# Queries and keys of an attention kernel as three bf16 terms instead of two f32r terms

## The chip, the cores and the metric

One NeuronCore of a Trainium2 chip runs one program. The metric is the device time of one execution in microseconds (us); of the kernel before, three executions are given.

## The reference

The input is x of shape 8 x 512 x 128 (batch, tokens, features), in f32. It passes two layers.

Layer 0: xn = layernorm(x), h = rmsnorm(xn). From h come q, k and v of 16 heads with 8 features each. There are two kinds of attention. The *linear* one is causal with the weight 1 + s + s²/4, where s is the product of 16 features made of q and of k; the *sliding* one is a softmax over the last 65 tokens, of q·k/sqrt(8). Their outputs, side by side, go through Wout. Beside them a feed-forward part runs on xn: silu(w1 x) * (w2 x), two hidden layers of 512 x 512 with gelu, and w3. The sum with x gives x1.

Layer 1: xn = layernorm(x1); *causal* softmax attention over the 512 tokens of a batch, 16 heads of 8 features, and beside it a choice of 2 of 8 experts for each token, each expert a 128-512-128 network with gelu, weighed by the softmax of the two logits. The sum of all is the output.

## The kernel before

**Scores.** All attention scores are made by `scores_into` (its matmul is L708): for a head and a block of 128 queries or keys, a matmul of 128 x 128 stationary against 128 to 512 moving columns. A head's keys stand in a buffer of 128 rows of which only its own rows are not zero, so the queries of several heads can lie in one 128-row block. To reach f32 precision a query and a key are each split in two f32r terms, high and low. A head takes 32 rows: three slots of 8 rows (high·high, low·high, high·low) and 8 rows of which one is used for minus the row maximum against a row of ones (the softmax shift). So 4 heads share a block of queries (`HG`), and Q1, QM, Q2 have 4 blocks of 512 tokens, K1 and K2b one block for each of 16 heads, all f32r (L298, L330). Q1 and K1 serve the sliding scores, QM and K1 the linear ones, Q2 and K2b the causal ones of layer 1.

**Splitting and moving.** ScalarE writes the high term (`split_hi`, L1111), VectorE subtracts it from the bank (`split_lo`, L1546). SyncE sends the terms to DRAM slot by slot (`split_and_send`, L516; `send`, L491), and ScalarE's queue sends those of q2 itself (L1244, L1248). From there SyncE fetches them into their slot rows (`fetch`, L498), for keys one DMA for each of the four head positions.
Row maxima are made ahead of the scores that use them: scores with queries as the stationary side, then a custom VectorE operation (`row_max`, L1579) reduces them; the table of maxima is transposed by TensorE, negated by `negate_max` (L1606) and put into the slot row by SyncE (`place_max`, L527).

**Stages.** Each batch of 512 tokens goes through a pairs stage, a slide stage and a dense stage; layers and batches are interleaved. In the pairs stage of batch b TensorE runs (`pairs_stage`, L834) the linear scores of batch b, row maxima for the causal scores of b-1 and for the sliding ones of b, the causal scores of b-1, and `weigh` (L766), the sums of values by heads, in bursts of 32 matmuls. ScalarE puts every score unit through exp or a square into `probs` (L1119), GpSimd masks them (L1308), VectorE does the maxima. A small bf16 sum over tokens, `prefix` (L826), counts the rows chosen for each expert. In the slide stage (`slide_stage`, L891) come the 32 sliding score units of b, and between them the projections of q, k and q·M for b+1 (q1, k1, qm1) and, from unit `GATES_AT` on, the 16 gate matmuls of the feed-forward part (L680). In the dense stage (`dense_stage`, L949) come the hidden layers for b+1 (`dense_low`, L701, 12 matmuls of 512 columns a unit, f32r terms high·high, low·high, high·low), and in the middle the end of layer 0 and the start of layer 1 for b: x1, its statistics, k2, q2, xnT, the expert logits and the choice.
The order on every engine is written out by hand. Seven PSUM banks are handed out in a ring; a unit waits until its bank was taken (`to_bank`), and an engine that reads a unit increments the bank's `taken` semaphore. In order of issue at the turn from layer 0 to 1: ScalarE writes high of k2, then of q2, then issues two sends of q2 (L1244), a gelu, and the third send. VectorE writes low of k2 and of q2 and then copies xnT, which TensorE's logits matmuls (L685) wait for.

**Parts.** The span has an opening (batch 0 only up to its queries and keys), batch 0 (`first`), six `steady` batches, a `last` batch without a following one, and a tail with the causal part of batch 7 and the expert tiles, which are sorted by expert (`stage_tile`, L1769, copies the weights of a tile's expert; L1782 copies its transposed input). In the opening SyncE fills the slot rows of ones (`set_slots`, `set_keys`, L482). Half of K1 and half of K2b double as room for the low parts of the hidden layers' weights and activations: SyncE loads these again from DRAM each batch (`load_low`, L512, L567 ff.) and GpSimd clears the room afterwards (`clear`, L1366, called in L1412 ff.). The expert weights W1 and W2 lie over Q1, QM and K1 (L331), so `load_experts` (L634) waits in the last batch for its last slide unit.

## Time and profile before

| | |
|---|---|
| median of three runs | 1272.86 us (1271.83 to 1275.03) |
| span of the profiled execution, first to last instruction | 1269.4 us |
| TensorE matmul (PE) busy | 1189.8 us, 94% |
| TensorE weight load (PEld) busy | 894.4 us, 70% |
| VectorE (DVE) busy | 848.0 us, 67% |
| ScalarE (ACT) busy | 734.5 us, 58% |
| GpSimd (POOL) busy | 665.2 us, 52% |
| DMA queues q1, q0, q10: packet time as a share of 16 engines | 25.2%, 5.3%, 2.0% |

A profile is of one execution; the profiled one has no device time of its own beside its span, so its span stands against the median of the runs, 3.5 us above it. The steady batch read here is that of 416.25 to 544.8 us; its pairs stage ends at about 476, its slide stage at about 509. In the rows, "PE bank L708" is a matmul of `scores_into`, "heads" one of `weigh`; K, Q, QM and W_s are names of whole groups of buffers. The chain of waits gives pieces in order of time, each followed back to what released it.

### The profile page before, as it was taken

The numbers are of one execution on the slowest core, as the hardware profiler recorded it, in microseconds if no ns is written. First come the engines' busy times: TensorE is split into PE (matmuls) and PEld (weight loads), VectorE is DVE, ScalarE is ACT, GpSimd is POOL, SyncE is SP. The second block draws the span as 40 slices with busy tenths as digits, with TensorE's granted clock in tenths as the row PEclk, the third lists the DMA queues.
The fourth block names the chain that finished last, engine by engine and source line by source line (L and its number), as shares of the span: only waits on it lengthen the run. The fifth ranks groups of instructions, "written<-read, shape, count | busy, mean of one in ns | idle before, by whom it ended". The sixth has DMA issues, their size and how long they took to land.

```text
span 1269.4 us, 26751 instructions
## 1 busy us (share of the span) xinstructions
PE 1189.8 (94%) x9122; PEld 894.4 (70%) x9122; DVE 848.0 (67%) x3390; ACT 734.5 (58%) x1561; POOL 665.2 (52%) x921
## 2 busy tenths in 40 slices
PE   5988999999999999999999999999999857989996
PEld 2566777677767776777677767776776657885896
DVE  4066597659865986588658855886588646874563
ACT  2356367736773577357745774567456524557674
POOL 4574364536443644464446444644465436675677
PEclk9999999999999999999999999999999968999999
DMA  7704420432043304230423043304330056541333
GB/s 219 210 3 162 132 77 12 158 123 92 13 160 109 106 14 159 96 120 13 158 97 119 13 151 105 117 15 137 118 117 15 11 151 147 81 66 25 45 55 39
DMA packets 88039, 119.30 MB, mean 94 GB/s; under 512 B 13736, under 2 KB 46416, under 8 KB 85904
## 3 DMA queue, kind: packets, MB, share of 16 engines
q1 hardware_dynamic: 69312, 99.66, 25.2%
q0 software_dynamic: 13792, 9.54, 5.3%
q10 hardware_dynamic: 4800, 8.39, 2.0%
q8 instruction: 73, 1.20, 0.4%
q14 instruction: 62, 0.51, 0.1%
HBM read 70.78 MB, written 48.46 MB: 94 GB/s over the span
## 4 chain that ended last, share of the span: by engine, by line
PE 63%; DVE 13%; ACT 10%; issue 6%; POOL 3%; DMA 3%; SPq 0%; DVEq 0%; POOLq 0%; ACTq 0%
PE bank L708 18%; PE heads L766 13%; PE bank L701 12%; PE bank L680 7%; ACT probs L1119 5%; PE bank L676 3%; PE bank L691 2%; DVE xnT_s L1579 2%; POOL out L1361 2%; PE bank L1054 2%; DVE hrow L1579 2%; DVE hT_s L1579 2%; PE bank L816 2%; PE bank L1062 1%; PE bank L685 1%
## 5 line engine op out<-in xcount | busy, mean ns | idle before, releaser
L1119 ACT ACTIVATE probs<-bank 128x512 f32<-128x512 f32 (+2 forms) x896 | 443.3, 578 | 186.5 <-PE bank L708 180.2
L1308 POOL TENSOR_SCALAR_AFFINE_SELECT probs<-probs 128x384 f32<-128x384 f32 x256 | 127.4, 520 | 211.7 <-ACT probs L1119 211.2
L708 PE MATMUL bank<-K,Q 128*128 128x192 f32 (+4 forms) x1024 | 236.5, 308 | 0.0
L708 PE MATMUL bank<-Q,K 128*128 128x192 f32 (+4 forms) x1024 | 220.7, 322 | 3.3 <-ACT probs L1119 3.1
L766 PE MATMUL heads<-probs,V 128*18 128x192 f32 (+9 forms) x3072 | 196.1, 396 | 6.6 <-POOL probs L1311 3.9
L708 PEld LDWEIGHTS bank<-K,Q 128*128 128x128 f32 x1024 | 166.5, 189 | 21.7 <-issue 9.6
L708 PEld LDWEIGHTS bank<-Q,K 128*128 128x128 f32 x1024 | 152.3, 194 | 39.5 <-issue 17.5
L766 PEld LDWEIGHTS heads<-probs,V 128*9 128x9 f32 (+1 forms) x3072 | 78.5, 94 | 114.0 <-issue 75.6
L1361 POOL DMA_INDIRECT out<-h1T_s x78 | 123.1, 1578 | 60.0 <-ACT h1T_s L1269 35.6
L708 PE MATMUL bank<-QM,K 128*128 128x512 f32 (+3 forms) x512 | 138.4, 336 | 4.6 <-ACT probs L1119 3.8
L1261 ACT ACTIVATE h2T_s<-bank,h1T_s 128x128 f32<-128x128 f32 x312 | 89.2, 368 | 91.8 <-PE bank L1054 88.9
L1320 POOL TENSOR_SCALAR_AFFINE_SELECT probs<-probs 128x512 f32<-128x512 f32 x64 | 54.9, 858 | 121.5 <-ACT probs L1119 121.1
L708 PEld LDWEIGHTS bank<-QM,K 128*128 128x128 f32 x512 | 85.2, 189 | 21.8 <-ACT probs L1119 6.2
L1369 POOL MEMSET K<- 128x512 f32 x120 | 57.1, 527 | 81.3 <-PE bank L701 80.9
L1054 PE MATMUL bank<-h1T_s,w_in 128*128 128x128 f32 x624 | 86.7, 284 | 0.0
L1579 DVE CUSTOM_DVE_ANT_0 hT_s<-bank,causal_neg_s 128x128 bf16<-128x128 f32 (+3 forms) x184 | 77.8, 455 | 13.1 <-PE bank L708 13.1
L1062 PE MATMUL bank<-w_out,h2T_s 128*128 128x128 f32 x624 | 83.9, 278 | 0.7 <-ACT h1T_s L1269 0.7
L1054 PEld LDWEIGHTS bank<-h1T_s,w_in 128*128 128x128 f32 x624 | 79.2, 199 | 0.8 <-issue 0.5
L1109 ACT ACTIVATE probs<-bank,sh_s 128x512 f32<-128x512 f32 x36 | 24.8, 688 | 94.8 <-PE bank L701 64.0
L1062 PEld LDWEIGHTS bank<-w_out,h2T_s 128*128 128x128 f32 x624 | 77.4, 195 | 0.8 <-ACT h2T_s L1261 0.8
L1348 POOL DMA_INDIRECT sorted_rows<-rows,slot_i x64 | 63.8, 998 | 16.5 <-issue 10.6
L1579 DVE CUSTOM_DVE_ANT_0 xnT_s<-bank,causal_neg_s 128x256 bf16<-128x256 f32 (+3 forms) x146 | 69.6, 502 | 4.0 <-PE bank L708 3.9
(224 smaller groups left out, 2184.9 us busy)
## 6 DMA issues: line engine op xcount, KB each, us to landing
Q<-slots_of_q SPq DMA_DIRECT2D x15, 1024.0 KB, 8.0
K<-low_of_h SPq DMA_DIRECT2D x13, 1024.0 KB, 7.8
QM<-slots_of_qm SPq DMA_DIRECT2D x8, 1024.0 KB, 6.0
K<-slots_of_k SPq DMA_DIRECT2D x60, 128.0 KB, 2.7
K<-slots_of_k SPq DMA_DIRECT2D x68, 96.0 KB
slots_of_q<-Q SPq DMA_DIRECT2D x24, 256.0 KB, 3.0
slots_of_k<-QM SPq DMA_DIRECT2D x24, 256.0 KB, 4.0
slots_of_qm<-Q SPq DMA_DIRECT2D x24, 256.0 KB, 4.2
```

The lines of the kernel that those rows point to most:

```text
L680: pe.matmul(to_bank(run, unit)[:, :], w, x, start=True, stop=True).then_inc(full_sem(run, unit), 1)
L701: mm = pe.matmul(to[:, :], left[:, n % FC, c * P:(c + 1) * P], right[n % FC], start=(n == 0), stop=(n == 3 * FC - 1))
L708: mm = pe.matmul(to[:, at:at + right.shape[1]], left, right, start=True, stop=True, skip_group_check=True)
L766: mm = pe.matmul(heads[ROWS * i:ROWS * i + n, P * j:P * j + widths[j]], V[:, j, g // 2, i, first:first + n], slot_of(kind, 2 * g + i // 2) ...
L1054: mm = pe.matmul(tile_hidden_bank(i)[:, c * P:(c + 1) * P], w_in[:, i % WB, c * P:(c + 1) * P], tile_xT[:, i % 2, :], start=True, stop=True)
L1062: mm = pe.matmul(tile_out_bank(i), tile_hidden[i % 2][:, c * P:(c + 1) * P], w_out[:, i % WB, c * P:(c + 1) * P], start=c == 0, stop=c == ...
L1119: return act.activation(to, bank, func, scale=scale, bias=bias).then_inc(taken_sem(run, unit), 1)
L1261: last = act.activation(tile_hidden[i % 2][:, c * P:(c + 1) * P], tile_hidden_bank(i)[:, c * P:(c + 1) * P], ACT.Gelu, bias=tile_b1[:, i % ...
L1308: pool.affine_select(out=three, in_=three, compare_op=ALU.is_ge, fill=0.0, base=0, pattern=[[0, 3], [1, P]], channel_multiplier=-1)
L1348: pool.indirect_dma_start(out=sorted_rows, out_offset=bass.IndirectOffsetOnAxis(ap=slot_i[:, n:n + 1], axis=0), in_=rows[:, n // K2, n % K ...
L1361: pool.indirect_dma_start(out=out.rearrange("b t d -> (b t) d"), out_offset=bass.IndirectOffsetOnAxis(ap=tile_rows[:, i % XB, P + 1:P + 2] ...
L1579: last = dve.tensor_tensor_reduce(beside[:, at:at + n], bank_of(run, unit)[:, at:at + n], mask, 1.0, NEG, ALU.add, ALU.max, to)
```

## The change

Queries and keys become three bf16 terms each. A head takes 64 rows: for each of 8 features six slots (pairs of terms with high·high, high·middle, middle·high, high·low, low·high, middle·middle) and two more for minus the maximum, itself now two bf16 terms. Two heads share a 128-row block (`SH`), Q1, QM and Q2 have 8 blocks in bf16, and K1 and K2b still 16, at half the bytes. After the high term (ScalarE) and the rest (VectorE, f32), ScalarE rounds the rest to the middle term (`split_mid`) and VectorE subtracts that for the low one (`split_low`). For k2 and q2 these stand in the dense stage, before VectorE's copy of xnT; for q1, k1 and qm1 in the slide stage, after unit 11 (ScalarE) and 13 (VectorE). Each term is sent by one DMA that writes it into one to three slots, and keys are fetched by two DMAs a half.
The low parts of the hidden layers stay in SBUF; their reload and GpSimd's clearing in every batch go. Expert weights lie over the unsplit gate and hidden activations (`whole_a`, `whole_b`), which are used last in the dense stage ahead of the last batch, and are loaded at the start of the last batch. The rows of ones come from a buffer of bf16 pairs, for all five at the opening.

```diff
+SG, SH = H // 2, 2
+SROWS = 64
+SLOT = 8
+AT_MAX = 6
+SLOTS_Q, SLOTS_K = ((0, 3, 1), (3, 5, 1), (5, 6, 1)), ((1, 6, 2), (0, 5, 4), (2, 3, 1))
+ONE_PAIR = 1.0 + 0x3F80 / 2 ** 23
...
-        Q2 = sb("Q2", [P, G, T], F32R)
+        Q2, K2b, K1 = sb("Q2", [P, SG, T], BF16), sb("K2", [P, H, T], BF16), sb("K1", [P, H, T], BF16)
         with ExitStack() as aside:
-            K2b = sb("K2", [P, H, T], F32R, aside)
-        whole_b = sb("whole_b", [P, H, T])[:, H // 2:H // 2 + FC, :]
+            low_a, low_h1, low_b, low_h2 = (sb(n, [P, FC, T], F32R, aside) for n in ("low_a", "low_h1", "low_b", "low_h2"))
+        W1, W2 = sb("W1_s", [P, E, T]), sb("W2_s", [P, E, FC, P])
...
+        def three(buf, first):
+            return buf[:, first, :], buf[:, first + 1, :], buf[:, first + 2, :]
+
+        def whole(buf, first):
+            return buf[:, first:first + 2, :].rearrange("p a t -> p (a t)").bitcast(F32)
+
+        parts_of = {"q1": three(Q2, 0), "qm1": three(Q2, 3), "k1": three(QM, 0), "q2": three(Q2, 0), "k2": three(Q2, 3)}
...
+        def by_slot(name):
+            return scratch[name].rearrange("h (d s) t -> (h d) s t", s=SLOT)
...
+            def set_slots(name, src):
+                sp.dma_start(by_slot(name)[:, AT_MAX:SLOT, :], src.rearrange("p (s t) -> p s t", t=T)).then_inc(S["slots_set"], 16)
...
+            def send(sequence, name, n):
+                sem = ("high", "mid", "low")[n]
+                sp.wait_ge(S[f"{sem}_{name}"], due(f"{sem}_{name}", sequence, 1))
+                sp.dma_start(slots_view(name, n), slots_src(name, n)).then_inc(S[f"sent_{name}"], 16)
...
-                    for i in range(HG):
-                        sp.dma_start(to[ROWS * i:ROWS * i + rows, HG * groups.start + i:HG * groups.stop:HG, :].bitcast(F32), by_row[i][0:rows, groups])\
+                    by_row = scratch[name].rearrange("(g i) r t -> i r g t", i=SH)
+                    for i in range(SH):
+                        sp.dma_start(to[SROWS * i:SROWS * (i + 1), SH * groups.start + i:SH * groups.stop:SH, :], by_row[i][:, groups])\
...
-                n = mrow.shape[0] // HG
-                for i in range(HG):
-                    row = ROWS * i + 3 * D
...
+                n = mrow.shape[0] // SH
+                for i in range(SH):
+                    for part in range(2):
+                        row = SROWS * i + AT_MAX + part
...
             def body(run, before, this, after):
                 part, b = run
+                if not after:
+                    load_experts()
...
                 if after:
                     for name in ("q1", "k1", "qm1"):
-                        split_and_send(run, (b, 1), name)
...
-                    load_low("h1", low_h1)
-                    if before:
-                        sp.wait_ge(taken_sem(run, CAUSAL_UNITS[-1]), taken_at(run, CAUSAL_UNITS[-1]))
-                        load_low("h2", low_h2)
-                    load_x((b, 1), (b + 2) & (NB - 1))
+                        send((b, 1), name, 0)
+                if after:
+                    for n in (1, 2):
+                        for name in ("q1", "k1", "qm1"):
+                            send((b, 1), name, n)
                 if before and this:
                     store(run, b - 1)
+                if this and after:
+                    load_x((b, 1), (b + 2) & (NB - 1))
                 if not after:
-                    load_experts(run)
...
                     sp.wait_ge(S["sent_k1"], due("sent_k1", (b, 1), SENT))
+                    fetch("k1", LOWER)
+                    fetch_sent((b, 1), "qm1")
                     fetch("k1", UPPER, "upper")
-                    fetch_sent((b, 1), "qm1")
                     fetch_sent((b, 1), "q1")
-                    if this:
-                        sp.wait_ge(S["keys1_restored"], due("keys1_restored", (b, 0), 1))
-                    fetch("k1", LOWER, restored=True)
                 if this:
-                    split_and_send(run, (b, 0), "k2")
+                    for n in range(3):
+                        send((b, 0), "k2", n)
...
                         fetch("k2", LOWER)
                         fetch_sent((b, 0), "q2")
-                        sp.wait_ge(S["keys2_restored"], due("keys2_restored", (b, 0), 1))
-                        fetch("k2", UPPER, "upper", restored=True)
+                        fetch("k2", UPPER, "upper")
...
-            def load_experts(run):
-
-                sp.wait_ge(taken_sem(run, SLIDE_UNITS[-1]), taken_at(run, SLIDE_UNITS[-1]))
+            def load_experts():
+
+                done = ("steady", LAST - 1)
+                sp.wait_ge(full_sem(done, "h1_3"), full_at(done, "h1_3"))
...
+            def split_mid(sequence, name):
+                act.wait_ge(S[f"rest_{name}"], due(f"rest_{name}", sequence, 1))
+                act.activation(parts_of[name][1], rest_of[name], ACT.Identity).then_inc(S[f"mid_{name}"], 1)
...
+                    if n == 11 and after:
+                        for name in ("q1", "k1", "qm1"):
+                            split_mid(nxt, name)
...
+                    split_high(run, now, "k2", bk1[:, 0:1])
+                    split_high(run, now, "q2", bq1[:, 0:1])
+                    split_mid(now, "k2")
+                    act.wait_ge(S["high_q2"], due("high_q2", now, 1))
+                    act.dma_start(slots_view("q2", 0), slots_src("q2", 0)).then_inc(S["sent_q2"], 16)
+                    split_mid(now, "q2")
+                    act.wait_ge(S["mid_q2"], due("mid_q2", now, 1))
+                    act.dma_start(slots_view("q2", 1), slots_src("q2", 1)).then_inc(S["sent_q2"], 16)
                     if after:
                         gelu(run, "h2_2", hidden_c[2], sh2[:, 2:3])
...
+                    act.dma_start(slots_view("q2", 2), slots_src("q2", 2)).then_inc(S["sent_q2"], 16)
...
-                if after:
-                    pool.wait_ge(full_sem(run, "h1_3"), full_at(run, "h1_3"))
-                    clear(K1, HALVES["k1"]).then_inc(S["keys1_restored"], 1)
...
-                if after:
-                    pool.wait_ge(full_sem(run, "h2_3"), full_at(run, "h2_3"))
-                    clear(K2b, HALVES["k2"]).then_inc(S["keys2_restored"], 1)
...
+            def split_rest(run, sequence, name, bias=None):
+                high, rest = parts_of[name][0], rest_of[name]
...
                 ins.then_inc(taken_sem(run, name), 1)
+                dve.wait_ge(taken_sem(run, name), taken_at(run, name))
+                dve.sem_inc(S[f"rest_{name}"], 1)
+
+            def split_low(sequence, name):
+                dve.wait_ge(S[f"mid_{name}"], due(f"mid_{name}", sequence, 1))
+                dve.tensor_tensor(parts_of[name][2], rest_of[name], parts_of[name][1], ALU.subtract).then_inc(S[f"low_{name}"], 1)
...
-                dve.tensor_scalar(mrow[:, :], bank_of(run, unit)[0:mrow.shape[0], 0:P], -1.0, None, ALU.mult).then_inc(taken_sem(run, unit), 1)
+                top = bank_of(run, unit)[0:mrow.shape[0], 0:P]
+                dve.tensor_scalar(mrow[:, 0, :], top, -1.0, None, ALU.mult).then_inc(S[sem], 1)
+                dve.wait_ge(S[sem], due(sem, sequence, nth))
+                dve.scalar_tensor_tensor(out=mrow[:, 1, :], in0=top, scalar=-1.0, in1=mrow[:, 0, :], op0=ALU.mult, op1=ALU.subtract)\
+                    .then_inc(taken_sem(run, unit), 1)
...
+                    if n == 13 and after:
+                        for name in ("q1", "k1", "qm1"):
+                            split_low(nxt, name)
...
-                    split_lo(run, now, "k2", bk1[:, 0:1])
-                    split_lo(run, now, "q2", bq1[:, 0:1])
+                    split_rest(run, now, "k2", bk1[:, 0:1])
+                    split_rest(run, now, "q2", bq1[:, 0:1])
+                    split_low(now, "k2")
+                    split_low(now, "q2")
```


## Rows read from the trace of the kernel before

**Rows 1.** Busy us (instructions) of PE, PEld, DVE, ACT, POOL; clock; DMA share; GB/s.

```profile
416.25:437.00 20.75, 20.68 (x160) 16.93 (x158) 19.62 (x105) 13.46 (x25) 15.72 (x26) 1.00 0.31 102
```

**Rows 2.** Chain of waits, steady batch, 417.5 to 546 us: start, length, what.

```profile
418.11 0.09 PE bank L826 x4
...
450.25 6.39 PE bank L708 x35
...
458.90 1.84 PE bank L708 x13
...
473.98 1.86 PE bank L708 x12
...
493.91 6.92 PE bank L680 x16
...
522.20 2.79 PE bank L701 x12
...
539.15 0.75 DVE Q L1552
539.90 0.61 DVE xnT_s L1544
540.56 1.06 PE bank L685 x8
```

**Rows 3.** VectorE's waits, 416 to 476 us: total, times, longest.

```profile
DVE hrow L1579 <- PE bank L708: 5.6, 4, 1.7
...
DVE xs L1838 <- issue: 0.4, 1, 0.4
```

**Rows 4.** Weight loads of lines 708 and 826: shortest, median, longest ns.

```profile
L708 PEld LDWEIGHTS bank<-K,Q x129: 186/188/192, 416.3 to 544.8; 128*128 128x128 f32 x129
...
L826 PEld LDWEIGHTS bank<-picks,ones x32: 95/98/105, 160.9 to 1065.9; 128*128 128x128 bf16 x32
```

**Rows 5.** Chain of waits, first batch, 57 to 77 us.

```profile
57.87 2.06 PE bank L708 x12
...
70.74 4.92 PE bank L708 x36
```

**Rows 6.** Groups by line and shape, whole span: busy us, mean ns.

```profile
L1798 DVE TENSOR_TENSOR K<-W_s,probs_high 128x512 fp32r<-128x512 f32 x28 | 26.7, 991 | 0.0
...
L1206 ACT ACTIVATE probs_high<-W_s 128x512 fp32r<-128x512 f32 x28 | 18.4, 655 | 0.0
```

**Rows 7.** ScalarE's timeline, 406 to 413.6 us (ACTq is its queue).

```profile
410.66 1.46 ACTq L1244 DMA_DIRECT2D slots_of_q<-Q  x2
```

**Rows 8.** VectorE's timeline: three stretches; in brackets the idle time before.

```profile
461.60 0.27 DVE L1608 TENSOR_SCALAR mrow_c<-bank 32x128 fp32r<-32x128 f32 x1
...
496.61 1.65 DVE L1793 SCALAR_TENSOR_TENSOR W_s<-bank,s_s,probs 128x512 f32<-128x512 f32 x2 [2.37 <-ACT probs L1109]
...
1033.20 0.16 DVE L1528 TENSOR_SCALAR pw<-mv 128x4 f32<-128x4 f32 x1
```

**Rows 9.** SyncE's timeline, 546 to 547 us.

```profile
546.42 0.38 SPq L506 DMA_DIRECT2D Q<-slots_of_q  x1
```

**Rows 10.** DMA issues, 544 to 553.5 us: KB each, us to landing.

```profile
Q<-slots_of_q SPq DMA_DIRECT2D x1, 1024.0 KB, 6.5
```

**Rows 11.** TensorE's timeline, 553 to 554 us.

```profile
553.37 0.44 PE L708 MATMUL bank<-K,Q 128*128 128x512 f32 x1
```

**Rows 12.** Page, DMA queues: packets, MB, share of 16 engines.

```profile
q1 hardware_dynamic: 69312, 99.66, 25.2%
...
q10 hardware_dynamic: 4800, 8.39, 2.0%
```

**Rows 13.** Chain of waits, last batch, 1019 to 1038 us.

```profile
1019.11 15.08 DMA W_s<-in_W
...
1037.13 0.34 DVE w_in L1775
...
1037.88 0.21 DVE h1T_s L1782
```

202 lines of the change are left out of this document (79 added, 123 removed), and 4 rows, old and new, of the table counts.

## Prediction

> **What bounds the kernel now.** I read the busy times of each stage first, then the chain of waits, then the lists by line. The unit to think in is one steady batch, 128.5 us long; six of them, a first and a last one and a tail make the span. TensorE is full in nearly every stretch. In the first one of the pairs stage VectorE is full too, 19.6 of 20.8 us [rows 1]: there the row maxima set the pace. The chain [rows 2] says where TensorE leads: after 447 us it runs in pieces of score matmuls between bursts of head sums. One piece is 6.39 us for 35 matmuls, then come six pieces from 458.90 to 473.98, together 81 matmuls in 11.41 us. VectorE sat idle only 5.6 us in four waits for these scores [rows 3], each just after a burst, so it is the close second there.
>
> **What the scores cost.** One score unit and one slide unit together are 3.6 matmuls and 864 columns. 81 matmuls are 22.5 such steps, 0.507 us each. The dense stage moves 12 matmuls of 512 columns in 2.79 us [rows 2], 0.454 ns a column, so the columns alone would need 0.392 us. The other 0.115 us is the weight load: every matmul has one, 188 ns long [rows 4], and behind a 128-column matmul it isn't hidden. A bf16 load of the same 128x128 takes 98 ns, and the four bf16 matmuls of the prefix passed in 0.09 us with a load each [rows 2].
>
> **The change, part by part.**
> 1. *Scores in bf16.* The number of matmuls and their columns stay (a key block is still 128 rows deep, two heads in place of four). What can go is the overhang: 22.5 x 0.115 = 2.6 us per pairs stage as the upper bound, nothing as the lower one. I take 1.8: the piece of 35 matmuls is held by VectorE (four waits only, continuous between), and in the others VectorE's maxima follow within two units. The stretch before 438 us is VectorE's and gives nothing but its wait of 0.4 us on the third layer [rows 3], since TensorE comes to it sooner. In the slide stage about four slide units lie just before the gate matmuls, 0.2 us; after the gates ScalarE leads and nothing is won. The first batch has no causal part and its three pieces (81 matmuls, 11.63 us, the first and the last in [rows 5]) have VectorE far behind: 2.1 us. The tail's causal scores run at ScalarE's pace: 0.
> TensorE's row for 512 columns against a page: the Trainium skill, TensorE: Matmul & The Clock Gate, Back-to-back issue gap, gives N/2.4 + 2.5 ns, 216 ns for 512 bf16 columns, where the dense row gives 232. It would add some 0.03 us a step, 0.6 us a stage. The same section gives about 81 ns for each 128-column matmul with its load in a sustained stream. That speaks against the change: it would leave about half of the overhang. The prefix row (four in 0.09 us) disagrees, though its matmuls are shorter.
> 2. *Third term of keys and queries 2.* This is the price. In the dense stage VectorE now forms the rest of k2 and q2 (0.75 us each) and then copies xnT, for which the logits matmuls wait: that is the chain at 539.15, 539.90 and 540.56 [rows 2]. The change puts two subtractions between them. A pass over 512 columns holds the chain for 0.61 us (539.90); the mean of such subtractions on SBUF is 0.99 us [rows 6], since most of them run beside GpSimd's masks. Beside that, the second one waits for ScalarE's middle term (0.65 us, the like in [rows 6]), which waits for the rest of q2 and stands behind a DMA issue (1.46 us for two [rows 7]). Step by step: rest q2 ends at 540.0, the first subtraction 540.7, middle q2 540.8, second subtraction 541.5, copy of xnT from there instead of 539.9: +1.6 us. Bounds 0.8 (the waits overlap) and 2.7 (2 x 0.99 + 0.73). Nothing covers it: logits, the last dense unit and the choice of experts follow in order on both engines, and VectorE then leads until 438. VectorE's wait for its own completion before it reports a rest has no row. The nearest is a handover: TensorE starts 0.05 us after xnT's end (539.90 + 0.61 to 540.56). There are two such waits, so 0.1; the ends are nothing and double that.
> 3. *The same for q1, k1, qm1 in the slide stage.* Three ScalarE copies (some 1.6 us) stand before slide units 12 to 15, three subtractions (2 to 3 us) before VectorE's first gate. ScalarE idles in between for a little less than that, so I take gate 0 to be evacuated 0.4 us later; VectorE sat idle 2.37 us before its gate [rows 8]. TensorE's 16 gate matmuls, 6.92 us [rows 2], set the end of the phase, and the banks they need are free by then. Cost 0. If that cover were gone, up to 1 us.
> 4. *Maxima as two terms.* One more operation like the 0.27 us one [rows 8] and a wait, three times a batch, two of them where VectorE is nearly full: +0.3. Placement takes as many DMAs as before, each row in two halves.
> 5. *DMA.* Sends carry the same bytes (six slots of 128 KB for three of 256 KB), in fewer ACT and SP issues of more, half-sized packets; a fetch of keys is two issues per half and not four. The two reloads of low parts, 2 MB a batch, go. Critical is the fetch of Q2: issued at 546.42, landed 6.5 us later at 552.9, used at 553.37 [rows 9 to 11]. Now everything on TensorE comes 1.6 us later, sends end about as before, and SP has two issues less ahead of the fetch: it is hidden with some 2 us to spare. Bound: the page gives 74 ns for the mean packet of the one queue (25.2% of 16 engines' 1269 us over 69312 packets of 1438 bytes) and 85 ns for the other's (2.0%, 4800 packets of 1748 bytes) [rows 12], both about 50 ns a KB. If a packet of 1 KB took 74 ns all the same, the fetch and the key half ahead of it, 1536 packets, would take 7.1 us and not 4.8, and land just too late. GpSimd's clears of the key halves go too; they were off the path.
> 6. *Expert weights.* Their load waited for the last slide unit and ended the chain with 15.08 us [rows 13]. Now it is issued a pairs stage earlier. But the weights weren't the only thing late: VectorE had its statistics until 1033.36 [rows 8], and the first transposed tile was copied only after two stagings, at 1037.88, the second of them 0.75 us long (from 1037.13) [rows 13]. With the weights there, two stagings from 1033.36 take 1.5 and the copy 0.2: 1035.1, 3.0 sooner. If the first staging stays as long as before (from 1034.19 to 1037.13), only 0.8 is won. Part of that length was register work that can now run ahead: I take -2.0.
> 7. *Opening.* Two more slot transfers ahead of the later weights, four key fills and a save less. I take 0. The ends are -1 and +2, a third of the 6.5 us that a megabyte took in [rows 10].
>
> **The sum.** Steady batch: -1.8 -0.4 -0.2 +1.6 +0.1 +0.3 = -0.4; six: -2.4. First: -2.1 -0.2 +1.7 +0.1 = -0.5. Last: -1.8 -0.4 -0.2 +0.3 +1.7 -2.0 = -2.4. Tail: two more small VectorE operations, +0.2. Together -5.1 us on the span of 1269.4. The median of the runs lies 3.4 us above that span (launch and end), which doesn't change: 1272.9 - 5.1 = 1267.8.
>
> **Rivals.**
> - *The splits cost more than the scores give* (slower). Place: ScalarE's middle term of q2 and VectorE's two subtractions ahead of xnT. At 2.7 us in place of 1.6 (+1.1 x 8) and with 0.8 us won in the pairs stage in place of 1.8 (-1.0 missing x 8): +16.8, 1284.6. It decides against the kernel once price less gain is 1.1 us a batch worse than I take (8.9 us from the forecast to 0.3% above the time before, over eight batches). For it: the 0.99 us mean, the DMA issue on ScalarE's queue, VectorE close behind TensorE. Against: at that very place the copy of xnT took only 0.61 us.
> - *bf16 loads gain nothing* (the change doesn't do what it says for TensorE: the overhang is something else, such as the wait for a free bank): all gains of part 1 gone but the last batch's weights: about +2.4 x 7 + 2.3 = +19, 1286.9; with half of it lost 1277.3. Against: the prefix row at 0.09 us. The sustained rate of the page named in part 1 comes near the half.
> - *More is won* (faster): the overhang goes in full (2.6, and the 6.39 us piece shrinks by 0.5), and the splits cost 1.0: seven batches by -1.9 and the first by -0.6 on top of the forecast, 1253.9. For it: VectorE's waits come after bursts, and a faster TensorE fills its banks before them.
> - *Q2 lands late*: at the packet price above 1 to 3 us in each of seven batches, +14: 1281.8. Against: the two queues' equal price per byte [rows 12].
>
> **How the numbers follow.** Forecast 0.44, more is won 0.20, splits cost more 0.16, bf16 gains half 0.10, nothing 0.04, late fetch 0.06. About 0.3% (3.8 us) is what a measurement of this kernel can tell from no change: 1269.0 to 1276.7 counts as the same. The forecast's own spread, 1261 to 1274, lies two thirds below 1269.0. Faster: 0.20 + 0.29 = 0.49; same: 0.15 from the forecast and 0.05 from the half gain, 0.20; slower: the rest, 0.31. The range leaves out a tenth at each end: 1253 to 1285.
>
> **What would show it.** In the changed trace: weight loads of the scores near 98 ns; a piece such as the 13 matmuls at 458.90 at 1.5 to 1.6 us and not 1.84; VectorE's waits after bursts shorter; the copy of xnT about 1.6 us later behind the rest of q2, and TensorE idle before the logits by as much more; gates starting as before; no wait on the slots of Q2 or K2; a steady batch of 128.1 us; no weight transfer in the chain of the last batch and its first tile some 2 us sooner. A batch over 129.5 us, or weight loads still near 188 ns, proves the forecast wrong; so does a batch under 126.5.

## The result, and the profile after

The changed kernel takes **1293.99 us** (median of 4 runs, 1291.48 to 1295.36) against 1272.66 us of the kernel before on the same chip (1271.83 to 1275.03): ratio 1.0161, 95% interval 1.0144 to 1.0178. It is slower by 1.6%, where 1267.8 was forecast with a range up to 1285. The spans of the profiled executions are 1293.6 and 1269.4 us, 24.2 apart; each execution's time is 1.7 to 2.0 us above its span, and the rest of the difference to 21.3 is spread among executions.

Of the page of the kernel after: span; busy time of each engine (share of the span) and instructions; DMA queues with packets, MB and share.

```profile
span 1293.6 us, 26679 instructions
...
PE 1169.2 (90%) x9122; PEld 753.7 (58%) x9122; DVE 873.8 (68%) x3454; ACT 753.1 (58%) x1601; POOL 610.9 (47%) x804
...
q1 hardware_dynamic: 102162, 85.89, 24.3%
...
q10 hardware_dynamic: 7872, 8.39, 1.9%
```

TensorE has 20.6 us *less* work in a kernel that is 24 us longer, although part of this work ran at half speed, as will be seen. The packets of the first queue grew in number by half and their share fell from 25.2% [rows 12] to 24.3%: the traffic as a whole is not the cause, and no DMA stands in the chain of the turn below.

**Where the time is, by stage.** These lengths are worked out from starts of matmuls in the traces, for the steady batch read before (b = 3). "Pairs" runs from the batch's first linear score to the transposes of hrow in the slide stage, so it holds the first five slide units too; "turn" runs from the transposes of hrow in the dense stage to the first linear score of the next batch.

| stage | before | after | |
|---|---|---|---|
| pairs | 66.57 | 65.54 | -1.03 |
| slide up to the gates | 10.92 | 10.63 | -0.29 |
| gates and rest of the slide stage | 15.34 | 15.31 | -0.03 |
| dense up to the turn | 25.81 | 27.20 | +1.39 |
| turn | 9.89 | 14.46 | +4.57 |
| batch | 128.53 | 133.14 | +4.61 |

Four of the profiled steady batches take 133.0 to 133.1 us, the last two 130.5 and 130.1. The six together give +21.9 us, the first batch +3.1 and the opening +0.8; the last batch and the tail are 1.6 us shorter.

**The turn.** The chain of waits of the kernel after, which answers to 539.15 to 544.5 in [rows 2]; the two rows of L1543 (DVE xs and Q) are the two rests, that of L1550 the two low terms:

```profile
551.33 0.76 DVE xs L1543
...
552.24 0.76 DVE Q L1543
...
553.14 1.29 DVE Q L1550 x2
554.43 0.61 DVE xnT_s L1535
...
555.09 1.88 PE bank L684 x8
556.97 5.18 PE bank L700 x12
```

The copy of xnT begins 6.53 us after the turn's start (547.90) where it was 5.01 before (534.89 to 539.90): +1.5, the term forecast at +1.6. What wasn't forecast stands in the last two rows. The eight logits matmuls take 1.88 us where they took 1.06 [rows 2], and h2_3's twelve take 5.18 where the kernel before had 2.90 (the twelve at 522.20 in [rows 2] took 2.79); of its chain:

```profile
541.61 2.90 PE bank L701 x12
```

The reason is in the windows. First the kernel after, then the one before: the stretch, its length, busy time of PE, PEld, DVE, ACT and POOL with instructions, granted clock, DMA share, GB/s.

```profile
429.22:450.00 20.78, 19.84 (x161) 11.30 (x159) 19.16 (x105) 13.61 (x26) 9.80 (x18) 1.00 0.27 67
512.78:520.70 7.92, 6.68 (x81) 4.74 (x79) 4.94 (x10) 7.91 (x19) 2.93 (x4) 1.00 0.23 68
520.70:524.30 3.60, 3.60 (x10) 2.84 (x11) 3.60 (x4) 2.39 (x5) 3.60 (x5) 0.53 0.25 72
...
552.80:555.00 2.20, 0.00 (x0) 0.00 (x0) 2.05 (x5) 1.32 (x3) 0.00 (x0) 1.00 1.00 339
555.00:561.90 6.90, 6.81 (x20) 5.51 (x20) 3.66 (x15) 0.00 (x0) 4.18 (x1) 0.51 0.67 186
```

```profile
501.00:509.00 8.00, 7.61 (x83) 6.56 (x81) 4.78 (x10) 7.88 (x19) 2.78 (x4) 1.00 0.65 232
509.08:512.70 3.62, 3.62 (x19) 3.08 (x20) 3.62 (x4) 2.46 (x5) 3.62 (x5) 1.00 0.27 80
...
539.50:540.60 1.10, 0.27 (x4) 0.08 (x2) 1.10 (x3) 0.00 (x0) 0.00 (x0) 1.00 0.88 229
540.60:544.80 4.20, 4.20 (x25) 3.65 (x26) 3.53 (x14) 0.94 (x2) 2.43 (x1) 1.00 0.97 301
```

Behind the wait for xnT (552.8 to 555.0, no matmul at all; TensorE's idle time before the logits is 2.4 us) the granted clock is 0.51 until 561.9, that is TensorE's lower level of 1.2 GHz and not 2.4. Before, the wait was 0.8 us and the clock stayed at 1.00. The same in a smaller way ahead of the dense stage. There ScalarE leads (7.9 us busy of 7.9), and TensorE with its faster scores is busy 6.68 of 7.92 us, before 7.61 of 8.00. The dense stage's first 3.6 us then run at 0.53: ten matmuls where there were nineteen. That is the +1.4 us of the dense row in the table. Summed over the six steady batches the trace's clock record has 47.8 us at the lower level in the kernel after and none in the kernel before. If TensorE filled all of it, half of that would be lost: 23.9 us as an upper estimate. In the batch of the table 4.5 us are read directly, 3.1 at the logits and h2_3 and 1.4 in the dense stage.

A page has this mechanism by name: the Trainium skill, TensorE: Matmul & The Clock Gate, section HAM oscillation, describes pauses of TensorE that bring on slow stretches, which repeat from tile to tile. The trace agrees that such stretches repeat (four batches in the same places). By its abstract rule on pauses, the one seen here would have been harmless; the measurement decides.

**The scores.** Weight loads and TensorE's own waits at the score line in the kernel after (ns: shortest, median, longest; below, us and times):

```profile
L707 PEld LDWEIGHTS bank<-K,Q x126: 95/98/100, 429.2 to 562.0; 128*128 128x128 bf16 x126
...
its engine sat idle before it (us, times) until:
  DVE mx_c L1575: 7.5, 20
  issue: 4.6, 18
  DVE mx_s L1575: 4.1, 14
```

and of the kernel before, of the lines under the same heading:

```profile
its engine sat idle before it (us, times) until:
  issue: 3.6, 16
  DVE mx_c L1579: 2.0, 8
```

The loads went from 188 to 98 ns as forecast. Worked out from start to start in the trace, the score matmul behind one of 512, 192 and 128 columns now starts after 216, 82 and 56 ns (medians at full clock, steady batches), where it was 285, 139 and 60; the overhang is gone in full, not by two thirds. The Trainium skill, TensorE: Matmul & The Clock Gate, section Wait — 56ns, not 53.3ns?, has these numbers for 128 and 512 columns, and the trace agrees. The 81 ns that the prediction cites from the Trainium skill are not seen. But the stage won 1.0 us and not 2.6: TensorE's idle time behind the row maxima (mx_c) rose from 2.0 us in 8 waits to 7.5 in 20. VectorE's waits, which answer to [rows 3]:

```profile
DVE hrow L1575 <- PE bank L707: 4.4, 4, 1.4
DVE hT_s L1575 <- PE bank L707: 2.4, 1, 2.4
DVE spare L1575 <- PE bank L707: 1.1, 1, 1.1
DVE xs L1838 <- issue: 1.1, 1, 1.1
```

Behind the bursts VectorE waits less than before (hrow 4.4 and not 5.6), while it has 1.3 us more work at the turn. Its one long new wait, 2.4 us for hT_s, stands at the batch's first maximum (429.31), behind the slow h2_3 of the turn, and its wait at the third layer is 1.1 us and not 0.4. So part of TensorE's gain has gone into waiting for VectorE.

### The profile page after: what moved, and what is told of

It reads as the page before. It is cut to its first block, busy times and chain, and to the rows that moved or that the text cites. A ratio compares the mean times of both kernels' runs of the same rounds, so it can differ in the third digit from the quotient of the medians.

```text
span 1293.6 us, 26679 instructions
## 1 busy us (share of the span) xinstructions
PE 1169.2 (90%) x9122; PEld 753.7 (58%) x9122; DVE 873.8 (68%) x3454; ACT 753.1 (58%) x1601; POOL 610.9 (47%) x804
## 3 DMA queue, kind: packets, MB, share of 16 engines
q1 hardware_dynamic: 102162, 85.89, 24.3%
## 4 chain that ended last, share of the span: by engine, by line
PE 51%; DVE 21%; ACT 13%; issue 7%; POOL 5%; DMA 1%; DVEq 0%; SPq 0%; POOLq 0%; ACTq 0%
PE bank L700 14%; PE heads L765 11%; ACT probs L1117 8%; PE bank L679 6%; PE bank L707 6%; DVE xnT_s L1575 4%; DVE hrow L1575 4%; DVE hT_s L1575 3%; PE bank L1050 2%; PE bank L690 2%; PE bank L1058 2%; POOL out L1362 2%; PE bank L675 2%; DVE spare L1575 2%; PE bank L684 1%
## 5 line engine op out<-in xcount | busy, mean ns | idle before, releaser
L1309 POOL TENSOR_SCALAR_AFFINE_SELECT probs<-probs 128x384 f32<-128x384 f32 x256 | 127.8, 521 | 241.7 <-ACT probs L1117 241.6
L707 PE MATMUL bank<-K,Q 128*128 128x192 bf16 (+4 forms) x1024 | 198.8, 271 | 4.1 <-ACT probs L1117 0.2
L707 PE MATMUL bank<-Q,K 128*128 128x192 bf16 (+4 forms) x1024 | 173.7, 273 | 16.8 <-ACT probs L1117 6.9
L707 PEld LDWEIGHTS bank<-Q,K 128*128 128x128 bf16 x1024 | 80.4, 98 | 88.2 <-ACT probs L1117 31.1
L707 PE MATMUL bank<-QM,K 128*128 128x512 bf16 (+3 forms) x512 | 121.5, 301 | 7.8 <-DVE gatesT_s L1535 1.4
L707 PEld LDWEIGHTS bank<-K,Q 128*128 128x128 bf16 x1024 | 84.9, 98 | 67.4 <-DVE mx_c L1575 14.6
L1329 POOL TENSOR_TENSOR rs<-pw,half_neg 128x4 f32<-128x4 f32 x32 | 32.5, 1028 | 158.9 <-DVE pw L1519 158.9
L1575 DVE CUSTOM_DVE_ANT_0 hT_s<-bank,causal_neg_s 128x128 bf16<-128x128 f32 (+3 forms) x184 | 77.8, 455 | 10.8 <-PE bank L707 8.7
L1058 PEld LDWEIGHTS bank<-w_out,h2T_s 128*128 128x128 f32 x624 | 78.5, 197 | 1.2 <-ACT h2T_s L1262 0.8
L1438 POOL TENSOR_TENSOR ex<-euler,lgs 128x32 f32<-128x32 f32 x8 | 44.8, 5604 | 60.3 <-DVE lgs L1644 60.3
L707 PEld LDWEIGHTS bank<-QM,K 128*128 128x128 bf16 x512 | 43.0, 97 | 49.1 <-DVE mx_c L1575 18.9
```

The costliest lines, as they stand in the source:

```text
L707: mm = pe.matmul(to[:, at:at + right.shape[1]], left, right, start=True, stop=True, skip_group_check=True)
L1058: mm = pe.matmul(tile_out_bank(i), tile_hidden[i % 2][:, c * P:(c + 1) * P], w_out[:, i % WB, c * P:(c + 1) * P], start=c == 0, stop=c == ...
L1309: pool.affine_select(out=three, in_=three, compare_op=ALU.is_ge, fill=0.0, base=0, pattern=[[0, 3], [1, P]], channel_multiplier=-1)
L1575: last = dve.tensor_tensor_reduce(beside[:, at:at + n], bank_of(run, unit)[:, at:at + n], mask, 1.0, NEG, ALU.add, ALU.max, to)
```

## The experiments

All rows of the table are worked out as above, in us; "turn + pairs" is from the transposes of hrow to the same point in the next batch's slide stage (before: 9.86 + 66.6). "Low" is the time at the lower clock within the six steady batches, and the last three columns go through these six as well. Each ratio is against the kernel before on the same chip, with its 95% interval.

| kernel | median | ratio | low | dense | turn + pairs | batch |
|---|---|---|---|---|---|---|
| before | 1272.66 | | 0 | 25.8 | 76.4 | 128.5 |
| after | 1293.99 | 1.0161 (1.0144 to 1.0178) | 47.8 | 27.2, two 25.8 | 79.8 to 80.0, one 78.4 | 133.1, two 130.1 and 130.5 |
| e1 dummy at the turn | 1277.85 | 1.0028 (1.0015 to 1.0040) | 17.1 | 27.2, one 25.8 | 76.8, one 77.2 | 128.9 to 130.3 |
| e2 low terms behind xnT | 1278.05 | 1.0030 (1.0015 to 1.0044) | 30.7 | 25.8 or 27.2 | 77.3, one 77.5 | 129.0 to 130.4 |
| e3 before, with delay | 1286.65 | 1.0095 (1.0075 to 1.0116) | 10.2 | 25.8 | 77.8, two 79.3 | 129.9, two 131.4 and 133.0 |
| e4 h2_3 first | 1279.24 | 1.0037 (1.0026 to 1.0049) | 20.5 | 25.8, one 27.2 | 77.3 to 78.4 | 129.6 to 130.5 |
| e5 dummy at both places | 1268.05 | 0.9963 (0.9949 to 0.9977) | 0 | 25.8 | 76.5 | 128.2 to 128.5 |
| e6 both, by moved work | 1268.98 | 0.9966 (0.9948 to 0.9985) | 6.8 | 25.8 | 76.0, two 77.5 | 127.7 to 129.3 |
| e7 before, h2_3 first | 1271.89 | 0.9991 (0.9977 to 1.0004) | 0 | 25.8 | 76.3 | 128.4 |
| e8 experts late | 1281.38 | 1.0061 (1.0044 to 1.0078) | 30.6 | 25.8, one 27.2 | 78.1, one 79.6 | 129.8, two 131.7 and 132.7 |
| e9 after, again | 1281.27 | 1.0072 (1.0045 to 1.0098) | 34.1 | 25.8 or 27.2 | 78.0 or 79.6 | 129.7 to 132.7 |
| e10 low terms by GpSimd | 1274.64 | 1.0016 (0.9997 to 1.0035) | 34.1 | 25.8 to 27.5 | 77.0 | 128.6 to 130.4 |
| e11 e10 and dummies | 1264.28 | 0.9941 (0.9923 to 0.9959) | 3.4 | 25.8, one 26.1 | 75.4 to 76.2, one 77.4 | 127.1 to 127.9, one 129.1 |
| e12 e2 and dummies | 1266.73 | 0.9950 (0.9933 to 0.9968) | 0 | 25.8 | 76.1 to 76.7 | 127.8 to 128.5 |
| e13 after, shifted | 1297.05 | 1.0194 (1.0172 to 1.0216) | 51.2 | 27.2, two 25.8 | 79.9 to 80.1, one 78.4 | 133.1, two 130.6 and 131.8 |
| e14 after, shifted more | 1299.94 | 1.0195 (1.0176 to 1.0214) | 58.0 | 27.2, one 25.8 | 80.0, one 78.5 | 133.1 to 133.4, one 131.7 |
| e15 after, a third time | 1294.65 | 1.0162 (1.0145 to 1.0179) | 58.0 | 27.2, one 25.8 | 80.0, one 78.5 | 133.1 to 133.5, one 131.8 |

e1 to e4 ran on one chip, e5 to e8 on a second, e9 to e12 on a third and e13 to e15 on a fourth. The unchanged kernel after was run only for the result above and as e9 and e15, and it took 1294, 1281 and 1295 us. So a total of e1, e2 or e4 can't be set against 1294 to the microsecond: what the same kernel would have taken on their chip isn't known. The lengths of the stages and the totals of one chip carry the argument.

**e1: is it the clock or the delay?** The same late xnT, with TensorE kept at work.

```diff
@@ dense_stage, TensorE
+                if after:
+                    for _ in range(8):
+                        pe.matmul(to_bank(run, "logits")[:, :], h2T[:, 0, 0:P], high_b[0], start=True, stop=True)
                 wait_taken(run, "xnT2")
                 project_rows(run, "logits", xnT, wgT[:, :], E)
```

> The kernel after, with eight added matmuls of 512 columns (their result is thrown away) that TensorE runs into the bank of the logits while it waits for xnT2, in all batches but the last. Theory (clock): the 2.4 us in which TensorE waits for xnT lower its granted clock, and the logits and h2_3 then cost 3.1 us more a batch (1.88 and 5.18 us for 1.06 and 2.90). Added work of about 1.9 us in that wait keeps the clock at 1.0, so the time falls by about 3 us in each of seven batches, to about 1273. Rival (delay): what costs is the later xnT on VectorE and what hangs on it; the added matmuls change nothing, 1294, or cost up to 1.9 us a batch, 1307.

Work was added and the kernel is faster, by 16 us against the first result; against the lower of the two levels of the kernel after (e9) it would be 3. Turn and pairs together take 76.8 us in all steady batches but one (77.2), 3.2 less than after: the clock's share, as the first theory had it. The unchanged kernel in e9 bears this out without a comparison of totals: its turn and pairs take 79.6 us at the three turns with 6.8 us at the lower clock behind the turn and 78.0 in the three with 3.4; here, with none, 76.8. In the windows of e1 the logits and h2_3 run at 1.00 (547 to 551), while the dip ahead of the dense stage, which this kernel doesn't touch, is still there in most batches:

```profile
504.56:512.47 7.91, 6.67 (x81) 4.73 (x79) 4.93 (x10) 7.90 (x19) 2.87 (x4) 1.00 0.25 68
512.47:516.00 3.53, 3.53 (x10) 2.81 (x11) 3.53 (x4) 2.46 (x5) 3.53 (x5) 0.55 0.20 54
...
547.00:551.00 4.00, 4.00 (x24) 3.31 (x25) 3.43 (x14) 0.11 (x1) 2.25 (x1) 1.00 0.44 154
```

**e2: the same cause taken away at its root.**

```diff
@@ dense_stage, VectorE
-                    split_low(now, "k2")
-                    split_low(now, "q2")
                     if not after:
                         run_tiles(MIXED, QUERIED)
                     take(run, "xnT2", xnT[:, :])
+                    split_low(now, "k2")
+                    split_low(now, "q2")
```

> The kernel after, with the two subtractions for the low terms of k2 and q2 behind VectorE's copy of xnT and not before it. Theory (clock): the copy of xnT comes 1.3 us sooner, TensorE's wait before the logits falls to about 1 us, which kept the clock at 1.0 before; so it wins 1.3 + 3.1 us a batch, together about -30 us if nothing else gives: about 1265, unless Q2 or K2 now land late. Rival (delay alone): -1.3 us in each of eight batches, 1283.

1278, where the theory had 1265 and the rival 1283. The total can't tell them apart, for the reason given under the table. Turn and pairs take 77.3 us, 2.7 less than after. xnT was on time, but shorter dips within h2_3 remained behind a wait of 1.2 us, and 30.7 us stayed at the lower clock. And the two subtractions cost VectorE their time behind the copy as well; see e12.

**e3: the delay alone, in the kernel before.**

```diff
@@ dense_stage, VectorE
                     split_lo(run, now, "q2", bq1[:, 0:1])
+                    if after:
+                        for to in (xs, hrow):
+                            dve.tensor_tensor(to[:, :, :], w3T[:, :, :], w3T[:, :, :], ALU.subtract)
```

> The kernel before, with two subtractions of 512 columns on VectorE (results unused) ahead of the copy of xnT, in all batches but the last: the length that the two low terms added, without bf16. Theory (clock): TensorE's wait grows from 0.8 to about 2.3 us, its clock falls and the logits and h2_3 lengthen: +1.5 +3 us in seven batches, about 1304. Rival (the clock falls because of bf16 scores or other parts of the change): +1.5 us in seven batches, 1283.

This run belongs to the rival in four of its six steady batches: each is 1.36 us longer (129.87 against 128.51) and keeps its clock over the same kind of wait, 2.0 of the 2.8 us of the first window below. Three of its seven turns dip, those of the first batch and of the last two steady ones: 12.6, 12.6 and 14.2 us for 11.1, by the same instructions and behind the same wait: TensorE's idle time before the logits is 2.04 us at all seven turns (2.41 in the kernel after, 0.83 in the one before).

```profile
549.00:551.80 2.80, 0.82 (x8) 0.82 (x8) 2.72 (x8) 0.69 (x1) 0.00 (x0) 1.00 0.97 281
551.80:555.20 3.40, 3.40 (x20) 2.87 (x19) 2.83 (x10) 0.24 (x1) 2.40 (x1) 1.00 0.76 255
```

Sum, as an estimate: 7 x 1.36 = 9.5, and the clock the rest of 12.9. So a wait of this length doesn't decide by itself, and neither does the kernel: this one meets it both ways. In the kernel after the clock fell at every turn. What else plays a part (less busy score stages, less work for PEld, other transfers, the place in time at which the wait falls) was not separated. That TensorE's lower share of work takes part is shown for the dip ahead of the dense stage (e5), not for the one at the turn.

**e4: filling the wait with work that has to be done anyway.**

```diff
@@ dense_stage, ScalarE: gelu of h2_2 from behind the sends of q2 to behind hT2
@@ dense_stage, TensorE
+                if after:
+                    dense_low(run, "h2_3", layer2, 3, range(8))
                 wait_taken(run, "xnT2")
                 project_rows(run, "logits", xnT, wgT[:, :], E)
                 if after:
-                    dense_low(run, "h2_3", layer2, 3)
+                    dense_low(run, "h2_3", layer2, 3, range(8, 3 * FC))
```

> The kernel after, with the first eight of h2_3's twelve matmuls ahead of the logits, and for that ScalarE's gelu of h2_2 (whose bank h2_3 takes) moved to just behind its evacuation of hT2. Nothing is added. Theory (clock): the wait of 2.4 us is filled with 1.9 us of work that had to be done anyway: its own length and the clock are won, 1.9 + 3.1 us in seven batches, about 1259. Rival (delay): only the moved work is won, at most 1.9 us a batch, 1281.

1279 and not 1259, next to the rival's 1281: the turn shrank to 9.5 us (from 14.5), less than before, and the pairs stage grew by about 3 us to 68.6. The wait has moved. VectorE leads from the turn up to the transposed gates, so work taken from behind the logits leaves TensorE idle in the first maxima, and there the clock falls now:

```profile
548.30:553.60 5.30, 3.66 (x26) 2.63 (x26) 4.70 (x23) 1.82 (x4) 3.47 (x1) 1.00 0.55 174
553.60:558.20 4.60, 4.47 (x28) 3.69 (x29) 4.16 (x28) 1.74 (x3) 4.43 (x7) 0.63 1.03 290
```

Real work that is only moved fills one gap and opens the next. The thrown-away matmuls of e1, which are extra, gave turn and pairs of 76.8 us, and this order 77.3 to 78.4.

**e5: the dip ahead of the dense stage.** e1, and from slide unit 17 on each unit's first score matmul twice (about 1.2 us).

```diff
@@ slide_scores, TensorE
+                if n >= 17:
+                    parts += parts[0:1]
                 scores_into(run, SLIDE_UNITS[n], parts)
```

> The run before with eight thrown-away matmuls at the turn, and besides from slide unit 17 on each unit's first score matmul issued twice into the same place, about 1.2 us more for TensorE in the 8 us ahead of the dense stage. There the kernel before had TensorE busy 7.6 of 8.0 us and the kernel after 6.7 of 7.9; after it the dense stage took 25.8 us before and 27.2 in most batches after, at a lower clock in its first 3.4 us. Theory (the faster scores leave TensorE too idle there): the dense stage takes 25.8 us in every batch, five of them shortened by 1.4: about 1271. Rival (the dips come from something else, such as the traffic of the DMAs): 1278 or more.

The dense stage takes 25.8 us in all batches, the lower clock is gone from all six, and the kernel is **faster than before** by 0.4%. On the same chip e8, the kernel after but for the load of the expert weights, took 1281.4, 13.3 us more. The windows answer to those of e1 above: 7.24 us busy of 7.74 and nineteen matmuls where there were ten.

```profile
498.22:505.96 7.74, 7.24 (x93) 5.84 (x92) 4.56 (x10) 7.73 (x19) 2.86 (x4) 1.00 0.25 68
505.96:509.50 3.54, 3.54 (x19) 3.01 (x20) 3.54 (x4) 2.46 (x5) 3.54 (x5) 1.00 0.21 51
```

**e6: e4's order with four matmuls, the low terms behind xnT, and e5's slide stage.**

> The kernel after with both low terms of k2 and q2 behind the copy of xnT, h2_2's gelu just behind hT2, four of h2_3's matmuls ahead of the logits, and the doubled slide matmuls of the run beside it. If late xnT and lowered clocks are the whole price, a batch keeps only the change's gains (1.1 us in the pairs stage, 0.3 around the gates): about 127.4 us a batch, 1264 in all, under the kernel before. Rival (VectorE's two subtractions cost their 1.3 us wherever they stand, since VectorE leads through the choice of experts and the pairs stage): 1273.

1269.0. Against e5 the turn is 2.1 us shorter (9.2) and the pairs stage 1.6 longer; VectorE leads in between. It is the middle between the two expectations (127.7 us a batch, but the first two steady ones 129.2 and 129.3).

**e7: is the order worth anything by itself?** The kernel before, with h2_2's gelu behind hT2 and four of h2_3's matmuls first.

> The kernel before with h2_2's gelu just behind hT2 and four of h2_3's matmuls ahead of the logits: what this order alone is worth. TensorE waited 0.8 us there. If VectorE leads from the turn to the middle of the pairs stage nothing is won: 1273. If TensorE leads, up to 0.8 us in seven batches: 1267.

No difference. VectorE leads from the turn to the middle of the pairs stage in the kernel before already, so TensorE's 0.8 us of waiting there costs nothing, as the first answer had it.

**e8: the expert weights.** Their load back behind the last slide unit.

```diff
@@ body, SyncE
-                if not after:
-                    load_experts()
...
                 if not after:
+                    sp.wait_ge(taken_sem(run, SLIDE_UNITS[-1]), taken_at(run, SLIDE_UNITS[-1]))
+                    load_experts()
```

> The kernel after with the expert weights loaded where they were loaded before, behind the last slide unit. The prediction took 2.0 us for the earlier load, between 0.8 and 3.0. So this run is 2 us slower than the kernel after, 1296; if the load was hidden either way or other waits take its place, 1294 as the kernel after.

The total can't be read: 1281.4, 12.6 *below* the kernel after, with steady batches whose instructions are the same. That opened the next question. The term itself shows in the stretch from the end of the slide stage to the first tile's matmul: 28.3 us here, 26.9 in e9, 28.4 in the kernel after's own profile, 29.3 before; so the earlier load is worth between nothing and 1.4 us, with the clock at 0.68 in that stretch in the kernels before and after alike.

**e9: the kernel after once more, unchanged.**

> The kernel after, unchanged. The run with the expert weights loaded late has the same instructions in its steady batches and yet took 129.8 us for four of them and 131.7 for one, where the kernel after took 133.1 and then 130.5. If the lowered clock depends on how a run happens to meet TensorE's waits, this run may show either: between 1279 and 1295. If the order of the expert load was what made the difference, it gives 1294 as before.

1281.3: "either" was right. The same program was at the lower clock for 47.8 us in one profile and for 34.1 in this. Its six steady batches are together 8.3 us shorter here, of which half of the 13.7 us explains 6.9.

**e13, e14, e15: what decides between 1294 and 1281?** The kernel after with two (e13) or five (e14) added matmuls in the opening, and beside them unchanged (e15).

```diff
@@ first_dense, TensorE
+                for _ in range(2):
+                    pe.matmul(to_bank(run, "v1")[:, :], hT[:, 0:P], hT[:, :], start=True, stop=True)
                 project_rows(run, "v1", hT, wv[:, :])
```

> The kernel after with two thrown-away f32 matmuls of 512 columns in the opening: up to 2 us once, and the same instructions in all batches behind. If the time depends on how TensorE's waits happen to meet the moments at which the granted clock changes, the batches fall into another pattern of lowered stretches, and the time differs from that of the unchanged kernel beside it by more than the 2 us, up or down. If the pattern belongs to the chip or the job, it is that of the kernel beside it plus at most 2 us.

> The same with five matmuls, up to 5 us once. Same reading: another pattern and a time more than some us away from the run beside it plus 5 us, or the same pattern.

> The kernel after, unchanged, on the chip of the two shifted ones. By its two results so far, either 1294 (batches of 133.1 us with 10.2 us of lowered clock each) or 1281 (batches of 129.7 to 132.7).

The three totals agree: 1294.7, and 2.4 and 5.3 us more for the shifted ones, as the added matmuls alone would have it. That looks like the end of the theory that it hangs on how a run meets its moments of clock, but in the place of the dips the shift didn't last. In all four profiles at this level (the kernel after, e13, e14, e15) at least four batches running keep step with the clock's record: one low stretch begins 0.1 to 0.7 us behind the start of the dense stage, the other 7.1 to 7.6 us behind the start of the turn, and each comes 133.12 us after that of the batch before, which is the batch's own length (133.1). The batches before these take other lengths and get there from wherever the opening left them (the first batch takes 103.7 to 105.4 us). So these runs say that a shift of the opening doesn't change the level; they don't say that the place of the dips doesn't matter. In e9 the record begins as in the kernel after: the low stretch of the first batch stands within 0.02 us of the start of the dense stage in both. One batch later it stands 0.5 us behind it and not 0.2, the next dense stage keeps its clock, and no such step sets in.

All four runs of the kernel in each of three jobs are alike (1291 to 1295, 1280 to 1285, 1294 to 1298), so something that belongs to the chip or the job decides whether the step sets in. Which of the two, and by what, stays open; in all three the kernel is slower than before, by 0.7 to 1.6%.

**e10: the low terms by GpSimd.** It was idle for 8.8 us at that point.

```diff
@@ dense_stage, VectorE
-                    split_low(now, "k2")
-                    split_low(now, "q2")
@@ body, GpSimd, behind y_init
+                for name in ("k2", "q2"):
+                    pool.wait_ge(S[f"mid_{name}"], due(f"mid_{name}", now, 1))
+                    pool.tensor_tensor(parts_of[name][2], rest_of[name], parts_of[name][1], ALU.subtract).then_inc(S[f"low_{name}"], 1)
```

> The kernel after with the low terms of k2 and q2 formed by GpSimd, which is idle for 8.8 us at that point. VectorE's chain from the turn to the transposed gates is then 1.3 us shorter than after, and nearly that of before. TensorE still waits about 1 us before the logits and is less busy ahead of the dense stage. Theory: turn and first half of the pairs stage together 1.4 us shorter than in the run with dummy matmuls, with one lowered stretch of clock (1.4 us) left in many batches: about 1272. Rival (GpSimd takes 2 us each for such work and Q2 comes late): 1280.

1274.6, about as the kernel before and 6.6 us below e9 on the same chip. Turn and pairs together take 77.0 us, not 1.4 less than with dummies as expected but 0.2 more, and 34.1 us at the lower clock are still in the six batches. GpSimd takes 1.15 us for each term (ns: shortest, median, longest):

```profile
L1436 POOL TENSOR_TENSOR Q<-xs,Q x2: 1152/1152/1153, 412.6 to 543.0; 128x512 bf16<-128x512 f32 x2
L1436 POOL TENSOR_TENSOR Q<-Q x2: 1150/1155/1160, 413.7 to 544.1; 128x512 bf16<-128x512 f32 x2
```

**e11: e10, four thrown-away matmuls ahead of the logits, and e5's slide stage.**

> The run beside it with four thrown-away matmuls before the logits and the doubled slide matmuls, which keep TensorE's clock up. If lateness on VectorE and the clock are the whole price: a batch of about 127.0 us, 1261 in all, faster than the kernel before by 0.9%. Rival (the pairs stage gives no more than 1.1 us and something else takes the rest): 1268.

**1264.3**, ratio 0.9941: the best of all, between the two expectations, and 8.7 us below the kernel before on the same chip. Five batches take 127.1 to 127.9 us; one still dips (129.1). This is the plainest proof of the clock's share: e10 and e11 ran on the same chip and differ in nothing but matmuls whose results are thrown away, and the run with more work is 10.4 us faster, with 3.4 us at the lower clock and not 34.1.

**e12: the same with the two subtractions on VectorE behind xnT.**

> The kernel after with both low terms of k2 and q2 on VectorE behind the copy of xnT, four thrown-away matmuls before the logits and the doubled slide matmuls. Against the run with GpSimd it differs by the place of 1.3 us of VectorE work. If VectorE leads from the turn to the transposed gates, it is 1.3 us slower in each of seven batches: about 1269. If TensorE leads there, both give the same, 1261.

1266.7 with batches of 127.8 to 128.5, on the mean 0.7 us over the five of e11 that keep their clock (128.1 against 127.4). So about half of VectorE's 1.3 us seems to be felt even behind xnT; the totals' intervals overlap and the batches' lengths nearly touch, so this is the weakest of these readings.

## Why the prediction was wrong

**The step that failed** is the sentence in part 2 "Nothing covers it: logits, the last dense unit and the choice of experts follow in order on both engines", with +1.6 us as the whole price. The delay itself came out at 1.5 us. But the sum put every later matmul at the speed of before. Behind the longer wait TensorE ran at half its clock for up to 6.9 us, which cost 3.1 us a batch (1.88 + 5.18 us for 1.06 + 2.90; 3.2 by e1), twice the delay. The second half is in part 1: what faster scores leave behind in a stage that ScalarE leads was taken as "nothing is won", and it was a loss of 1.4 us in four of six batches, which extra work for TensorE took away (e5). None of the four rivals had the clock in it, although the trace of before could have told of it: from 1008.7 to 1038.2 us, where its last batch waited, the granted clock was 0.68:

```profile
1008.70:1038.20 29.50, 17.58 (x169) 14.53 (x169) 13.42 (x33) 7.36 (x18) 11.50 (x13) 0.68 0.57 167
```

The prediction's own sign of being wrong, a steady batch over 129.5 us, holds for all six (130.1 to 133.1). On the chip of e9 the same kernel takes 1281.3 us, within the range; that would have been luck, for the clock that makes it so is in no term of the range.

Point by point, per steady batch:
- *Scores in bf16*: the forecast was that two thirds of the overhang go, 1.8 us in the pairs stage, and 0.4 at the third layer. All of the overhang went (56 ns from start to start at 128 columns), but turn and pairs without dips won little: 76.5 in e5 against 76.4 before, with 1.3 us more for VectorE; 75.4 in the best three batches of e11 without that, so about 1.0 us is what the faster scores are worth. The third layer's wait grew to 1.1 us. Mechanism right, size under half: TensorE's idle time behind mx_c rose by 5.5 us, so VectorE was closer behind than "four waits only" suggested.
- *Third term at the turn*: +1.5 for +1.6, right; what it set off, missed.
- *Split in the slide stage, maxima as two terms*: 10.6 us up to the gates against 10.9, and the sixteen gate matmuls start within 6.49 us in both kernels. Cost 0 was right for the split. The second term of a maximum takes VectorE 0.31 us more each time (457.49 to 457.80), 0.9 a batch; how much of that is felt, +0.3 by the forecast, was not separated.
- *DMA*: no wait on slots of K2 or Q2 stands in the chain; and a packet of the first queue now takes 49 ns (24.3% of 16 engines' 1293.6 us over 102162 packets of 841 bytes), where it took 74 in the kernel before: roughly in step with its size, 58 ns a KB for 51. The fetch of Q2 took 8.4 us and not 6.5 (issued at 559.13), and landed about 3 us before its first use at 570.74. Hidden, as forecast, though a longer fetch.
- *Expert weights*: the forecast -2.0, with -0.8 as the far end if the first staging stayed long. VectorE's timeline of the kernel after shows the two stagings (1058.22 and 1059.23) taking from 1057.45 to 1061.07, 3.6 us for the forecast 1.5:

```profile
1057.29 0.16 DVE L1519 TENSOR_SCALAR pw<-mv 128x4 f32<-128x4 f32 x1
1058.22 0.43 DVE L1775 COPY w_in<-W_s 128x512 f32 x1 [0.78 <-issue]
...
1059.23 0.43 DVE L1775 COPY w_in<-W_s 128x512 f32 x1
1059.58 1.25 DVE L1776 COPY h1T_s<-b_s 128x4 f32 x1
...
1061.07 0.28 DVE L1782 COPY h1T_s<-bank 128x128 f32<-128x128 f32 x1
```

  The stretch to the first tile became 0.9 us shorter (29.3 to 28.4), near the far end.
- *The turn of the last batch*: forecast +1.7 with its waits. From the turn's start to the logits it is +2.1 (6.64 to 8.71 us). From the first tile's matmul to the first score of the tail it is +4.0 (27.7 to 31.7), with the granted clock 0.86 and not 0.91; the rest was not separated. It ate most of what the last batch and the tail won elsewhere.
- *The tail's causal scores*: forecast "at ScalarE's pace: 0". From the first to the last of their weight loads they take 26.1 us for 26.9, and the row maxima and tiles ahead of them 79.3 for 81.7, which the forecast had at +0.2 (why stays open). The chain of before went through score matmuls there, that of after through ScalarE. First before, then after:

```profile
1150.33 6.95 PE bank L708 x23
...
1160.76 3.35 PE bank L708 x11
```

```profile
1177.01 2.32 ACT probs L1117 x5
...
1179.40 2.17 ACT probs L1117 x4
```

## What to carry to other kernels

A delay on another engine is priced twice when TensorE waits for it: once by its length, and again if the granted clock falls behind the wait; here 1.5 us of delay cost 3.1 us more (less than half of that in some batches of e9), and TensorE was full on both sides. So look up the clock of every stretch before and after a wait that a change makes longer, and in a stage that TensorE doesn't lead, treat a faster matmul as a longer idle time and not as free. If such a wait can't be removed, a microsecond or two of thrown-away matmuls in it may pay (e5, e11), while moving real work into it only moves the gap when another engine leads (e4). And a kernel whose clock dips has to be timed on more than one chip, beside its own control.

## What had not been expected of the hardware

- The wait that brings on a lower clock in one kernel doesn't always in another: 2.41 us without a matmul at each of the seven turns of the kernel after, all with a dip; 2.04 us at each of the seven turns of e3, with a dip at three.
- One program, unchanged, has two levels by chip or job, each steady to 0.4%: 1294 and 1281 us, with 47.8 or 58.0 against 34.1 us at the lower clock in the profiles, while the kernel before stays within 1272.3 to 1273.9 in its medians everywhere.
- At the slower level the loop keeps step with its own dips: four low stretches or more follow each other 133.12 us apart with batches of 133.1 us, and 2 to 5 us more in the opening don't change that.
- bf16 score matmuls hide their weight load altogether: 56, 82 and 216 ns from start to start at 128, 192 and 512 columns (medians), where the f32r ones had 60, 139 and 285.
